# Taking a skip term off TensorE and reordering who copies a PSUM bank first, in a chunked recurrent scan

## The reference

```python
xr, gate = split(x @ W_in.T)              # 1024 wide each
xr = xr + t_emb                           # per batch
xc = silu(causal_conv_4_taps(xr) + b_conv)
xn = layernorm(xc) * ln_g + ln_b
Bm, Cm, dt = split(xn @ W_xproj.T)        # 16 states each
dt = tanh(dt @ W_dt.T + b_dt) * 0.01
Ad = 1 - dt * tanh(A_log);  Bd = Bm * min(norm(xn), 1)
h  = clip(h * Ad[:, None] + Bd[:, None] * xn[None, :], -10, 10)   # 16 x 1024 state, token after token
y  = sum over states of Cm * h  + D * xn  # D * xn is the skip term
out = x + (y * silu(gate)) @ W_out.T
```

## Time and profile before

| | |
|---|---|
| median of 3 runs | 2062.3 us (2061.71 to 2063.79) |
| the profiled execution | 2062.99 us, its span 2061.2 us |
| busy: PE, PEld | 1871.3 us (91%), 1417.4 us (69%) |
| busy: DVE | 1602.5 us (78%) |
| busy: ACT | 1379.5 us (67%) |
| busy: POOL | 1746.4 us (85%) |
| granted TensorE clock | 0.987 of full over the span |

### The profile page before, as it was taken

One profiled execution on the slowest core, in us unless ns is written; L12 is line 12 of the kernel. 1 busy time (PEld: TensorE's weight loads), 2 busy tenths in 40 slices (PEclk: granted clock), 3 DMA queues, 4 the chain that ended last, 5 costly groups with the idle time before them and its releaser, 6 DMA issues.

```text
span 2061.2 us, 46097 instructions
## 1 busy us (share of the span) xinstructions
PE 1871.3 (91%) x16368; PEld 1417.4 (69%) x16368; DVE 1602.5 (78%) x2045; ACT 1379.5 (67%) x3462; POOL 1746.4 (85%) x1444
## 2 busy tenths in 40 slices
PE   5589999999999999999999999999999999999988
PEld 5466776767776766776776776676776676777655
DVE  3387787878887878887888887877887787878786
ACT  4577666777666677667677666777766776766653
POOL 1388888899888889988889988889988889988896
PEclk9699999999999999999999999999999999999999
DMA  5222222222222222222222222232222222222221
GB/s 177 58 56 60 70 63 64 73 59 68 75 58 67 68 64 66 73 58 71 65 72 61 69 58 73 62 75 62 67 57 76 62 77 59 67 62 72 57 68 31
DMA packets 168068, 139.14 MB, mean 68 GB/s; under 512 B 100704, under 2 KB 137968, under 8 KB 163168
## 3 DMA queue, kind: packets, MB, share of 16 engines
q1 hardware_dynamic: 167840, 136.20, 24.8%
HBM read 62.07 MB, written 9.31 MB: 35 GB/s over the span
## 4 chain that ended last, share of the span: by engine, by line
PE 52%; ACT 17%; issue 15%; DVE 10%; SPq 2%; POOL 2%; DMA 1%; DVEq 0%; ACTq 0%; POOLq 0%
PE ps_y L599 11%; PE ps_job L516 8%; PE ps_job L482 7%; DVE ks L997 6%; PE ps_fill L563 6%; PE ps_fill L572 6%; PE ps_job L495 4%; ACT tap L759 3%; ACT low L801 3%; PE ps_y L579 3%; PE ps_job L489 3%; ACT xh L697 2%; PE ps_job L486 2%; ACT lend L779 1%; ACT gate L691 1%
## 5 line engine op out<-in xcount | busy, mean ns | idle before, releaser
L997 DVE TENSOR_TENSOR_SCAN ks<-low,ps_fill 128x512 f32<-128x512 f32 x1024 | 1211.3, 1208 | 267.6 <-PE ps_fill L572 267.2
L1095 POOL TENSOR_TENSOR prod<-ks,crep 128x512 f32<-128x512 f32 x1024 | 1285.6, 1273 | 157.3 <-DVE ks L997 131.0
L801 ACT COPY low<-ps_fill 128x512 f32<-128x512 f32 x1024 | 584.5, 580 | 518.0 <-PE ps_fill L563 515.4
L599 PE MATMUL ps_y<-c_sb,prod 128*128 128x128 f32 x4096 | 610.2, 274 | 1.8 <-POOL prod L1095 1.0
L599 PEld LDWEIGHTS ps_y<-c_sb,prod 128*128 128x128 f32 x4096 | 458.6, 141 | 80.3 <-issue 43.7
L563 PEld LDWEIGHTS ps_fill<-ts,xs 128*128 128x128 f16 x4096 | 314.4, 98 | 176.5 <-issue 9.9
L572 PE MATMUL ps_fill<-spans,pick 128*128 128x512 f16 x1024 | 390.2, 381 | 46.8 <-ACT low L801 46.8
L563 PE MATMUL ps_fill<-ts,xs 128*128 128x128 f16 x4096 | 397.1, 220 | 13.2 <-DMA xs<-h 7.3
L759 ACT ACTIVATE tap<-xr,cols_sb 128x128 f32<-128x128 f32 x768 | 251.8, 393 | 0.0
L477 PE MATMUL ps_job<-x,w_in 128*128 128x128 f16 x3072 | 215.4, 221 | 10.3 <-POOL x L1065 7.8
L482 PE MATMUL ps_job<-w_in,x 128*128 128x512 f16 x768 | 203.3, 381 | 21.3 <-ACT gate L691 21.3
(11 more groups left out here) (123 smaller groups left out, 2003.1 us busy)
## 6 DMA issues: line engine op xcount, KB each, us to landing
crep<-c_dram SPq DMA_DIRECT2D x32, 1024.0 KB, 4.8
xs<-xh SPq DMA_DIRECT2D x256, 64.0 KB, 2.0
xs<-xl SPq DMA_DIRECT2D x224, 64.0 KB, 2.0
xf<-in_xT SPq DMA_DIRECT2D x32, 256.0 KB, 2.8
res<-in_x SPq DMA_DIRECT2D x32, 256.0 KB, 2.7
out_dram<-res SPq DMA_DIRECT2D x32, 256.0 KB, 2.3
ts<-tth SPq DMA_DIRECT2D x128, 32.0 KB
ts<-tth SPq DMA_DIRECT2D x128, 31.0 KB
```

Of the source, the lines that this page charges most:

```text
L599: last = mm(ps_y[:, cut], prod[:, (TILES * k + s) % HOLD, e, :], ident, start=False, stop=(u % 4 == 3 and q == 3 and e == QN - 1), is_tran ...
L801: copy(low[:, (TILES * k + s) % RING], ps_fill[:, (TILES * k + s) % RING]).then_inc(sem["low_copied"], 1)
L997: nc.vector.tensor_tensor_scan(ks[:, u % 2, QN * q:QN * (q + 1)].rearrange("d n t -> d (n t)"), low[:, g % RING], ps_fill[:, g % RING], 0. ...
L1095: tt(prod[:, g % HOLD], ks[:, u % 2, part], crep[:, p, part], ALU.mult).then_inc(sem["weighed"], 1)
```

## The change

The skip term leaves PE. POOL makes D * xn in two halves, into the first half of `xc` and a new tensor `y1`, whose bytes also serve as the second `y16`; POOL waits beforehand until the transposes of the older `y16` have landed. DVE adds it as y leaves `ps_y`, and multiplies by the gate in a second instruction, in place in the job bank. A new semaphore `y_summed` after the addition frees `ps_y` for `base`, and `xc` for the convolution.

In the carry, DVE's instruction no longer waits for ACT's copy to `lend`. ACT makes that copy at the next point, after DVE's instruction, and this copy now frees the bank for the next job and for `gated`. Five of the eight tap blocks move.

```diff
-        TAP_AT = [24, 28, 30, 34, 38, 40, 43, 46]
+        TAP_AT = [24, 28, 33, 38, 40, 42, 44, 47]
...
# bank_free
-                    pe.wait_ge(sem[name + "_taken"], (kk + off) * per + i + 1)
+                    freed = "lend_set" if name == "carry" else name + "_taken"
+                    pe.wait_ge(sem[freed], (kk + off) * per + i + 1)
...
# PE
-                since(pe, "y_gated", 2 * k + i)
+                since(pe, "y_summed", 2 * k + i)
                 mm(ps_y[:], mT[:, p], xn[:, p, half], start=True, stop=False)
-            def skip(k, p, i):
-                if i == 0:
-                    pe.wait_ge(sem["xd_done"], k + 1)
-                last = mm(ps_y[:], ident, xd[:, i * BANK:(i + 1) * BANK], start=False, stop=False)
-                if i == 1:
-                    last.then_inc(sem["xd_used"], 1)
...
-                if s in (3 * NQ, 4 * NQ):
-                    skip(k, p, s // NQ - 3)
...
# ACT: xc of the convolution
-                    since(act, "xd_used", k + 1)
+                    if i == 0:
+                        since(act, "y_summed", 2 * k + 1)
...
# ACT: carry
                     copy(ch[:, half], bank("carry", i)).then_inc(sem["carry16"], 1)
+                for i in range(2):
+                    if point != TAKE["carry", i] + 1 or not exists(k, 1):
+                        continue
+                    half = slice(i * BANK, (i + 1) * BANK)
+                    act.wait_ge(sem["carry_taken"], 2 * (k + 1) + i + 1)
                     if exists(k, 0):
                         act.wait_ge(sem[f"lend_in{p}"], 16 * pair(k, p, 0))
                     copy(lend[:, half], bank("carry", i)[0:NS]).then_inc(sem["lend_set"], 1)
...
# DVE: carry
-                    dve.wait_ge(sem["lend_set"], 2 * j + i + 1)
...
# DVE: gated
+                dve.wait_ge(sem["xd_done"], 2 * k + i + 1)
+                bank_free(dve, k + i, [job[2:4] for job in JOBS].index(("yT", i)))
+                tt(bank("yT", i), ps_y[:], xd[i], ALU.add).then_inc(sem["y_summed"], 1)
                 dve.wait_ge(sem["gate_taken"], 2 * k + i + 1)
-                bank_free(dve, k + i, [job[2:4] for job in JOBS].index(("yT", i)))
-                tt(bank("yT", i), ps_y[:], gate[:, half], ALU.mult).then_inc(sem["y_gated"], 1)
+                dve.wait_ge(sem["y_summed"], 2 * k + i + 1)
+                tt(bank("yT", i), bank("yT", i), gate[:, half], ALU.mult).then_inc(sem["y_gated"], 1)
...
# POOL, tile 11
-                        tt(xd[:], xn[:, p], row_d[:], ALU.mult).then_inc(sem["xd_done"], 1)
+                        since(pool, "yT_in1", N_YT * k)
+                        for i in range(2):
+                            half = slice(i * BANK, (i + 1) * BANK)
+                            tt(xd[i], xn[:, p, half], row_d[:, half], ALU.mult).then_inc(sem["xd_done"], 1)
```

More of the change, by code:

```diff
@@ L79 @@
 halo_saved conv_taken stats aggr rstd moments z0 zb ad scan_p recip weighted bound32 bound16 bound_all p_kept
-norm_in xa xg xn_done xh_done xl_done yT_high squares root nrm nb16 tt_done xd_done xd_used kend_done c_out c_in
+norm_in xa xg xn_done xh_done xl_done yT_high squares root nrm nb16 tt_done xd_done y_summed kend_done c_out c_in
 y_gated yT_in0 yT_in1 carry16
@@ L182, in build @@
         ones = gate[:, 0:P]
-        xd = xc
         res = sb("res", [P, DM])
-        y16 = [gate[:, 0:BANK].bitcast(H).rearrange("t (a d) -> t a d", a=2), sb("y16", [P, 2, BANK], H)[:]]
+        y1 = sb("y1", [P, BANK])
+        y16 = [half.bitcast(H).rearrange("t (a d) -> t a d", a=2) for half in (gate[:, 0:BANK], y1[:])]
+        xd = [xc[:, 0:BANK], y1[:]]
         ps_fill = S.enter_context(nc.psum_tensor("ps_fill", [P, RING, BANK], F))
```

## The result

The changed kernel takes 2059.23 us (median of 14 runs, 2056.58 to 2060.68), the kernel before 2063.64 us on the same chips (14 runs, 2061.1 to 2064.72). The ratio is 0.998, with a 95% interval of 0.9972 to 0.9987: 4.4 us faster where I forecast 2.2 us slower. The profiled execution took 2057.65 us around a span of 2055.9.

The account below looks back on a forecast made before the run. PE paces the kernel, ACT the stretch changed. Bodies 1 to 29 +2.9 us, body 0 +0.1, body 30 -0.86, body 31 +0.2: sum +2.3 on 2062.3, called 2064.5 us, no change; range 2044 to 2076.

Parts of the forecast that it names:

- The bound: PE paces the kernel overall, but where the change acts ACT, not PE, is short of time.
- Part 1: Two skip matmuls of 0.86 us leave PE per body; the first gains nothing, the second 0.86 us if followers are ready.
- Parts 2 and 3: DVE's extra addition, about 0.7 us per half, mostly hidden; POOL's D * xn in halves, 0.1 us more.
- Part 4: At the carry ACT waits for DVE, its conv take comes 0.90 us later and stops PE: +0.10 us a body.
- Body 0: It already has the take's wait, then a 2.54 us DMA wait hides the change: +0.1 us.
- The last two bodies: Body 30 gains one skip, -0.86 us; body 31 gains a skip but pays an uncovered multiplication, +0.2 us.
- Rival 1: Faster: ACT's take of conv half 0 is not late, 24 us gained, 2038 us; chance 0.22 with its larger form.
- Rival 2: Slower: TensorE's clock falls in PE's new stop before flip 19, +12 to +46 us; chance 0.08.
- Rival 3: Slower: ACT's list slips further, each stop costing 0.2 us more, +9 us, 2071 us; chance 0.14.
- Rival 4: DVE becomes the bound through 44 us more work, +41 us, 2103 us; chance 0.04.
- PE's busy time: Sign that the forecast is right: it falls by about 55 us while the span stays.

Follow-up runs that it names:

- e3: The changed kernel with one tap block moved from point 44, ahead of ACT's take of conv half 0, to 45, behind it: 2023.06 us, ratio 0.9806.
- e8: The kernel before without its two skip matmuls and nothing in their place, so y lacks D * xn: 2039.57 us, ratio 0.9882.
- e1: The changed kernel with the two waits of DVE's carry instruction swapped, making the one for ACT's copy a separate entry: 2063.04 us, ratio 1.0003.
- e2: The kernel before with DVE's wait for the lend copy put first, so the instruction itself carries it: 2057.26 us, ratio 0.9974.
- e11: The changed kernel with tap points 24, 32, 37, 38, 40, 45, 46, 48: 2000.37 us, ratio 0.9694.
- e5: The kernel before with the eight tap points of the changed kernel and nothing else: 2038.93 us, ratio 0.9880.
- e9: The kernel before with tap points 24, 28, 33, 38, 40, 45, 46, 48, its skip matmuls and carry order kept: 2025.84 us, ratio 0.9816.
- e6: The kernel before with only the D term moved to DVE, carry order and tap points unchanged: 2059.22 us, ratio 0.9974.
- e7: The kernel before with only the new carry order, DVE ahead of ACT's lend copy: 2056.03 us, ratio 0.9962.
- e12: The changed kernel with the tap points of the kernel before: 2059.64 us, ratio 0.9981.

## Why the prediction was wrong, point by point

I forecast 2.2 us slower, called it no change, and the kernel came out 4.4 us faster.

**The bound: right.** "In the stretch where the change acts, ACT is the engine that is short of time." e3 shows it: 36 us from one tap block.

**Part 1: right.** The first skip became a wait (e8), the second is on the path only if nothing stops PE behind it. In after the stop takes it back.

**Parts 2 and 3: right in size.** The addition takes 675 ns in half 0 and 700 ns in half 1; `base` waits for it 0.2 us a body; POOL's two halves start 1.23 us apart and take 0.13 us more than the one instruction of the earlier trace rows.

**Part 4: the mechanism was right, and its hand-over term was mis-sized. This is the step that failed.** I took 0.14 us from ACT's end to DVE's start out of a row in which the late wait was a separate entry. In after it measured 0.04 and 0.03 us. ACT's two new waits are 1051.12 - (1050.17 + 0.47) = 0.48 and 1055.32 - (1053.94 + 0.47) = 0.91, together 1.39 us and not 1.59. The take came 1063.37 - 1049.23 = 14.14 us after the same tile copy, before it was 13.45: +0.69 where I had +0.90. `base` came 7.83 us after it, forecast 8.00. Flip 19 came 14.76 us after it; before had 14.94 and my forecast was 15.00. That is -0.18, and the slower restart (0.49 us to the next start against 0.44) gives 0.05 back: -0.13 a body by these rows, -0.12 by the bodies, where I took +0.10. Over 29 bodies that is -3.5 in place of +2.9.

e1 puts the slow hand-over back and nothing else, and my sum comes out: the take 14.31 us after the tile copy (forecast 14.35), `base` 7.99 (8.00), flip 19 14.93 (15.00), the ratio 1.0003 (forecast 1.0011, inside the interval). The same hand-over also lengthens four bodies of before by 0.35 us each (experiment 2). They are gone in after: another -1.3 us that my sum did not have.

```profile
1066.40 0.66 PE L591 MATMUL ps_y<-c_sb,prod 128*128 128x128 f32 x4 [1.62 <-ACT xc L759]
```

This is flip 19 in PE's timeline of e1, 14.93 us after the tile copy at 1051.47.

The stop of PE was 1.61 us, where my times gave 1067.97 - 1065.85 = 2.12: it needed 1062.22 - 1057.06 = 5.16 us from `base` to that point and I had 4.88. That had no price, since the take sets flip 19.

**Body 0: wrong by 1.4 us.** I took the 2.54 us wait for a DMA as a cover for the change. Its cost was the clock: 0.52 granted behind it. After has a longer stop and nearly the same one, PE's timeline 144 to 160 us:

```profile
146.17 0.66 PE L591 MATMUL ps_y<-c_sb,prod 128*128 128x128 f32 x4 [3.00 <-ACT xc L759]
...
155.69 0.38 PE L565 MATMUL ps_fill<-ts,xs 128*128 128x128 f16 x4 [2.05 <-DMA xs<-h]
```

and the full clock behind the second (window, busy time of each engine, granted clock, DMA share, GB/s):

```profile
158.00:161.00 3.00, 3.00 (x33) 2.61 (x32) 2.35 (x3) 2.79 (x5) 2.00 (x1) 1.00 0.02 5
```

**The last two bodies: wrong by 1.5 us, +0.84 where I had -0.66.** Three large pieces, all in timelines of after (the rest is -0.26). In body 31 PE stood 1.77 us for POOL's product at 2016.96, and then ran at 0.51:

```profile
2016.96 0.66 PE L591 MATMUL ps_y<-c_sb,prod 128*128 128x128 f32 x4 [1.77 <-POOL prod L1098]
```

```profile
2018.20:2021.40 3.20, 3.20 (x16) 2.53 (x17) 2.21 (x2) 1.19 (x3) 3.20 (x3) 0.51 0.00 0
```

In before a skip stood in this stretch (at 2021.55), PE had no idle time above 0.5 us there, and the granted clock was 1.00. From y's half at 2006.40 and 2000.44 to the next one it takes 20.89 in before and 22.15 in after, +1.26. The uncovered multiplication of the last half was as forecast, from 2042.69 to 2044.85 is 2.16 us, against 1.35 behind the earlier trace rows, +0.81:

```profile
2042.69 0.70 DVE L982 TENSOR_TENSOR ps_job<-ps_y,y 128x512 f32<-128x512 f32 x1 [0.83 <-PE ps_y L591]
...
2044.85 0.69 DVE L915 SCALAR_TENSOR_TENSOR y<-ps_job,y 128x512 f16<-128x512 f32 x1 [0.65 <-ACT y L675]
```

The last 24 output matmuls took 6.96 us on the chain in place of 7.93, because the low clock lasted for the first 3.3 us of them rather than 5.2 (to 2048.97 from their start at 2045.68, in before to 2054.95 from 2049.71): -0.97. The skip's 0.86 us in body 30 brought nothing, because the chain doesn't lie on PE there in either kernel. The chain of after, 1955 to 2000 us:

```profile
1974.80 1.04 POOL ttl L1081
1975.86 0.67 SPq L407
...
1987.38 3.85 DMA xs<-h
...
1991.48 0.38 PE ps_fill L565 x4
```

POOL's products lead to SP's stacking DMAs, these land, and PE's fill starts: the same path as in e11. From the scan to `ttl` it takes 20.09 us, in before 1980.79 - 1960.85 = 19.94.

The errors of body 0 (-1.4) and of the last two bodies (+1.5) nearly cancel. That is luck: neither was foreseen.

**The rivals.** Rival 1 was half right: faster, and the exchange between ACT and DVE cost less than I counted, but the take did not stay. Rival 2's mechanism happened once, at the place above, for 1.3 us; it did not happen in bodies 1 to 29, which have a stop of 1.61 us each and a granted clock of 1.00 from 178 to 1950 us. The Trainium skill's rule on short gaps ("TensorE: Matmul & The Clock Gate", section "A second HAM failure mode: psum-queue depth-cycling") would let one expect these bodies to swing; the trace disagrees here too. Rival 3 did not happen: the stops were shorter than I counted, and even e1 stays level with before. Rival 4 did not happen: DVE is busy 80%.

**PE's busy time** fell by 38.9 us and not by 55. The records of the skips overlap those of the matmuls beside them, which accounts for a part; how much is not shown.

**Open.** The long bodies go with the separate wait: bodies 5, 13, 21 and 29 are long by this hand-over in before, e5, e8 and e9 (body 5 of e8 by 1.7 us more, for another reason), body 17 alone is in e1 and e6, and none is in e2, e7, e12 and after, where the late wait is carried. Why it is just these bodies, nothing here shows. Why a stop of 1.77 us lowers the clock in body 31 and one of 3.00 us in body 0 doesn't is open as well. The division of the gain was read from one profiled execution of each kernel; that the order of waits is worth some 6 us (e2 against before) rests on timed runs.

## What to carry to other kernels

Before crediting a change with the wait that it removes, find the next point at which the sped-up engine meets the engine that pays, and ask whether the payer's list before that point grew: here three edits worth 5, 8 and 25 us alone were worth 4 together, and moving one piece of filler behind that meeting point released 36. When forecasting a hand-over from a row, check that the wait will stand at the same place in the instruction's list of waits; and put the wait that comes last first in the source. Where a sum of small distances decides between a gain and a loss, a term of 0.1 us used twice in each of 29 bodies is the whole forecast.

## What the runs showed of the hardware

- A wait that comes last costs 0.03 to 0.04 us from the producer's end to the start when the instruction carries it, and 0.11 to 0.14 us when it is an entry ahead of it (after and e2 against before and e1), and 0.47 to 0.51 us in a few bodies: every eighth one in before. By e2 and e1 that is 6 us and 4 us of the whole.
- ACT's starts follow 0.47 us apart for instructions of 0.57 us, and DVE's pair with a wait between them (addition, multiplication) starts 0.78 us apart at 0.68 to 0.70 us each. The wait for the addition thus costs about 0.1 us plus the lost overlap (the scan behind the multiplication, with no such wait, starts 0.61 us after it). It is the second wait in the source and an entry of its own in the chain (DVEq L984 at 2043.43), so part of the 0.1 us may be that entry's; no run separates the two.
- The clock fell to 0.51 behind a stop of 1.77 us at 2016.96, and stayed at 1.00 behind stops of 3.00 and 2.05 us in body 0 and of 1.61 us in the bodies between. In before it fell to 0.52 behind one of 2.54 us. The length of the last stop alone does not tell which it will be.
